# A graph network of eight layers on one core: node stages in chunks of four tiles, layer norm by the statistics instruction, batch norm in one round, counts a step later

## The reference

```python
# block 0: one layer, mean of the neighbours
agg = segment_sum(h[src], dst) / maximum(count(dst), 1)
x = x + relu(h @ W_self.T + agg @ W_neigh.T + bias)
# block 1: an edge filter, and the product of the messages at each node
bf = exp(coeff * (dist[:, None] - centers) ** 2)
bf = ssp(ssp(bf @ W1 + b1) @ W2 + b2)              # ssp(z) = softplus(z) - ln 2
msg = h[src] * edge_feat * bf * cut[:, None]
x = x + ssp(segment_prod(msg, dst) @ W3 + b3)
# block 2: three layers of  mean(h[src]) @ Wl + h @ Wr + b, relu between them
x = x + third_layer
# block 3: three attention layers, each followed by leaky relu and batch norm
out = segment_sum((h @ W)[s] * coef[:, None], d) + bias     # coef: softmax over each node's edges
h = batch_norm(leaky_relu(out, 0.01))              # mean and variance over the 6250 nodes
x = x + h
```

## Time and profile before

| | us |
|---|---|
| median of three runs | 9773.72 (9766.58 to 9774.74) |
| the profiled execution, its own time | 9773.36 |
| its span, first to last instruction | 9771.3 |
| TensorE matmuls busy | 4612.8 (47%) |
| VectorE busy | 5238.5 (54%) |
| ScalarE busy | 1189.0 (12%) |
| GpSimd busy | 6513.7 (67%) |
| mean granted TensorE clock | 0.632 of full speed |

### The profile page before, as it was taken

One profiled execution on the slowest core, in us unless ns is written; L12 is line 12 of the kernel. 1 busy time (PEld: TensorE's weight loads), 2 busy tenths in 40 slices (PEclk: granted clock), 3 DMA queues, 4 the chain that ended last, 5 costly groups with the idle time before them and its releaser, 6 DMA issues.

```text
span 9771.3 us, 95144 instructions
## 1 busy us (share of the span) xinstructions
PE 4612.8 (47%) x25947; PEld 3624.8 (37%) x25947; DVE 5238.5 (54%) x15043; ACT 1189.0 (12%) x1461; POOL 6513.7 (67%) x6626
## 2 busy tenths in 40 slices
PE   0433447777733334433443336635267353572543
PEld 0433333333333334433343335335254253442533
DVE  3455457777753333333343336957359583395844
ACT  0000017777720000000000001000010000100001
POOL 0666747777757776777677773777737777377774
PEclk9655567777765656655565555566565675655756
DMA  1211224444421122121221121233112331123321
GB/s 57 61 45 45 64 55 123 125 124 124 119 68 52 52 52 56 52 52 52 52 56 52 52 53 58 90 112 97 39 55 89 103 110 47 40 76 114 116 55 30
DMA packets 525925, 702.75 MB, mean 72 GB/s; under 512 B 121707, under 2 KB 392050, under 8 KB 524444
## 3 DMA queue, kind: packets, MB, share of 16 engines
q0 software_dynamic: 211680, 414.97, 16.3%
q1 hardware_dynamic: 299224, 230.52, 7.8%
q10 hardware_dynamic: 14688, 53.48, 1.4%
HBM read 552.58 MB, written 145.94 MB: 71 GB/s over the span
## 4 chain that ended last, share of the span: by engine, by line
POOL 52%; issue 21%; PE 13%; DVE 11%; SPq 1%; DMA 1%; ACT 0%; DVEq 0%; POOLq 0%; ACTq 0%
POOL rows L651 26%; POOL rows L681 22%; PE PS L1018 5%; DVE T L1457 2%; PE PS L1050 2%; PE PS L980 2%; POOL nd L664 1%; POOL at_first L657 1%; SPq L459 1%; DVE acc L1334 1%; PE PS L1043 1%; DVE H L1362 1%; PE PS L906 1%; DVE onehot L1316 1%; DVE H L1364 1%
## 5 line engine op out<-in xcount | busy, mean ns | idle before, releaser
L651 POOL DMA_INDIRECT rows<-table,src_t x3920 | 3899.9, 995 | 1874.7 <-issue 1216.6
L1334 DVE TENSOR_TENSOR acc<-acc,PS 128x128 f32 x5488 | 1559.6, 284 | 3383.5 <-PE PS L980 2141.2
L681 POOL DMA_INDIRECT rows<-table,src_t x2352 | 2268.5, 964 | 1137.5 <-issue 753.7
L980 PE MATMUL PS<-onehot,rows 128*128 128x128 f32 x6272 | 1451.5, 425 | 2119.2 <-DMA rows<-table,src_t 2119.2
L980 PEld LDWEIGHTS PS<-onehot,rows 128*128 128x128 f32 x6272 | 1350.3, 327 | 2208.6 <-DMA rows<-table,src_t 2208.6
L1009 PE MATMUL PS<-onehot,rows 128*128 128x128 f32 x3072 | 688.5, 415 | 1197.5 <-DMA rows<-table,src_t 1142.8
L1009 PEld LDWEIGHTS PS<-onehot,rows 128*128 128x128 f32 x3072 | 637.0, 316 | 1242.2 <-DMA rows<-table,src_t 1192.2
L1403 DVE TENSOR_SCALAR onehot<-PS,loc_t,ex_t 128x128 f32<-128x128 f32 x2352 | 943.8, 403 | 0.5
L1018 PE MATMUL PS<-H,mats 128*128 128x512 f32 x784 | 514.8, 794 | 8.9 <-DVE H L1436 6.6
L1316 DVE TENSOR_TENSOR onehot<-PS,loc_t 128x1024 f32<-128x1024 f32 x392 | 477.0, 1218 | 6.4 <-DMA table<-H 5.8
L1092 PEld LDWEIGHTS PS<-als_bf,onehot 128*128 128x128 bf16 x7056 | 308.3, 119 | 426.0 <-DVE onehot L1569 269.6
(11 more groups left out here) (308 smaller groups left out, 5372.8 us busy)
## 6 DMA issues: line engine op xcount, KB each, us to landing
rows<-table,src_t POOLq DMA_INDIRECT x6272
staged<-rows ACTq DMA_DIRECT2D x102, 512.0 KB
H<-staged SPq DMA_DIRECT2D x102, 512.0 KB
prod_rows<-onehot SPq DMA_DIRECT2D x98, 512.0 KB, 3.3
G<-in_edge_attr SPq DMA_DIRECT2D x97, 512.0 KB, 4.2
table<-H SPq DMA_DIRECT2D x49, 448.0 KB
G<-perm_rows SPq DMA_DIRECT2D x4, 3136.0 KB, 12.1
cut_row<-flat_bf SPq DMA_DIRECT2D x294, 2.0 KB
```

What stands on the lines that cost most here:

```text
L651: pool.indirect_dma_start(rows[:, j, :], None, table[k % 2], at(src_t[:, t:t + 1]))\
L681: pool.indirect_dma_start(rows[:, g % 2 * HT + j, :], None, table[k % 2], at(src_t[:, t:t + 1]))\
L980: last = mm(PS[:, o:o + D], rows[:, r, :], onehot[:, r, :], start=True, stop=True)
L1334: tt(at, at, PS[:, h * 1024 + j * D:h * 1024 + (j + 1) * D], ALU.add).then_inc(added[h], 1)
```

## The change

Four things are changed together.

1. **Chunks.** CH goes from 7 to 4, so that a chunk is 512 elements, one PSUM bank. There are 13 chunks, the last of one tile, everywhere: node stages, table stores, output stores, the node products of every layer. In the attention layers the turned rows, the products and `mid` get two buffers each, and `turn_rows(c + 1)` is issued ahead of `multiply_rows(c)`. Each layer has a semaphore of its own for its table chunks.
2. **Layer norm.** `layer_input` and the old `normalize` go. `row_moments` takes mean and variance of a tile with `bn_stats` and `bn_aggr`, one of each for every tile, on VectorE. ScalarE takes the square root of the chunk's variances, or, behind layer 1, exp(-0.5 ln v), which VectorE refines by one Newton step. VectorE makes scale and shift for each node (`shift_rows`), and ScalarE writes relu(scale * x + shift) tile by tile (`normalized_rows`). The norm of chunk c - 1 is finished behind the moments of chunk c. The input of layer 0 goes through the same chunks.
3. **Attention outputs and batch norm.** The bias is added to all of T in `self_weights`, by a second operation over it, and the self weight is divided by the softmax sum there. The output of a chunk is then a product, a sum and the leaky relu. Batch norm subtracts the mean of the first chunk in place of the mean of all nodes, sums and squares are summed on TensorE in the same round as the outputs (`first_sum`, `statistics` inside `to_nodes`), and the closing arithmetic makes scale and shift from them. A last round applies them.
4. **Counts a step later.** VectorE's digits start at step 16 instead of 15, and TensorE multiplies the digits of step c in step c + 1. Likewise the facts and the permutations move by a step.

The core of the diff:

```diff
-CH = 7
-NCH = NT // CH
+CH = 4
+NCH = -(-NT // CH)
...
-COUNT_FROM = 15
+COUNT_FROM = 16
...
+            def normalized_rows(k, c):
+                nonlocal n_norm
+                n_norm += 1
+                s.wait_ge(norm_ready, n_norm)
+                for t in tiles_of(c):
+                    last = nc.scalar.activation(H3[:, t, :], X3[:, t, :], ACT.Relu, bias=shift_n[:, t:t + 1],
+                                                scale=rstd_n[:, t:t + 1])
+                last.then_inc(h_chunks[k], 1)
...
+                    after_ranks(k, c - 1)
+                after_ranks(k, NCH - 1)
+                after_ranks(k, NCH)
+                if k in GAT:
+                    deviation(bn[:, 3 * D:4 * D], bn[:, 3 * D:4 * D])
+
+            def after_ranks(k, c):
+                if k in (0, 4):
+                    normalize(k + 1, c)
+                if k in GAT and 0 <= c < NCH:
+                    s.wait_ge(sum_in, (k - 5) * (NCH + 1) + c + 2)
+                    nc.scalar.activation(flat(G, c), flat(H, c), ACT.Square).then_inc(squares, 1)
+
+            def normalize(k, c):
+                if 0 <= c < NCH:
+                    inverse_deviation(k, c)
+                if 1 <= c <= NCH:
+                    normalized_rows(k, c - 1)
...
             def rows_product(k):
                 turn_rows(k, 0)
                 for c in range(NCH):
-                    multiply_rows(k, c)
                     if c + 1 < NCH:
                         turn_rows(k, c + 1)
+                    multiply_rows(k, c)
...
                     move_ranks(c)
+                    if k in GAT:
+                        if c == 0:
+                            first_sum(k - 5)
+                        if c > 1:
+                            statistics(k - 5, c - 2)
+                if k in GAT:
+                    statistics(k - 5, NCH - 2)
+                    statistics(k - 5, NCH - 1)
...
                     if k == 0:
-                        if COUNT_FROM <= c < FACTS_AT:
+                        if COUNT_FROM < c <= FACTS_AT:
                             for q in range(2):
-                                count_nodes(2 * (c - COUNT_FROM) + q)
-                        if c == FACTS_AT:
+                                count_nodes(2 * (c - 1 - COUNT_FROM) + q)
+                        if c == FACTS_AT + 2:
                             sum_facts()
-                        if PERM_FROM <= c < PERM_FROM + PERMS:
-                            turn_perms(c - PERM_FROM)
+                        if PERM_FROM < c <= PERM_FROM + PERMS:
+                            turn_perms(c - 1 - PERM_FROM)
...
+            def row_moments(c):
+
+                six = moments[:].rearrange("p (t q) -> p t q", q=6)
+                for j, t in enumerate(tiles_of(c)):
+                    last = nc.vector.bn_stats(six[:, j, :], X3[:, t, :])
+                step(last)
+                for j, t in enumerate(tiles_of(c)):
+                    last = nc.vector.bn_aggr(mean_var[:, t, :], six[:, j, :])
+                step(last, var_ready)
...
+            def shift_rows(c, by_log):
+                w = slice(c * CH, c * CH + len(tiles_of(c)))
+                inverse_taken()
+                if by_log:
+                    r, x, two = rstd_n[:, w], shift_n[:, w], mean_var[:, w, 1]
+                    step(stt(x, two, EPS, r, ALU.add, ALU.mult))
+                    step(stt(x, x, -0.5, r, ALU.mult, ALU.mult))
+                    step(stt(r, x, 1.5, r, ALU.add, ALU.mult))
+                else:
+                    step(recip(rstd_n[:, w], rstd_n[:, w]))
+                step(stt(shift_n[:, w], mean_var[:, w, 0], -1.0, rstd_n[:, w], ALU.mult, ALU.mult), norm_ready)
+
+            def normalize(c, by_log=False):
+                if c < NCH:
+                    row_moments(c)
+                if c > 0:
+                    shift_rows(c - 1, by_log)
...
+                step(tt(exs_n, exs_n, rden_n, ALU.mult))
                 step(tt(T3, T3, exs_n.unsqueeze(2).broadcast_to([P, NT, D]), ALU.mult))
+                step(tt(T3, T3, vec_nodes(bias_vec[k]), ALU.add))
...
+                outputs(0)
+                outputs(1)
                 v.wait_ge(sum_out, 2 * l + 1)
-                step(ts(nm, PS[:, 0:D], -1.0 / N, None, ALU.mult))
...
+                step(ts(minus_first, sums_ps, -1.0 / (CH * P), None, ALU.mult))
+                centred(0)
+                centred(1)
+                for c in range(2, NCH):
+                    outputs(c)
+                    centred(c)
                 v.wait_ge(sum_out, 2 * l + 2)
```

345 lines of the change are left out of this document (169 added, 176 removed).

## The result

The changed kernel takes 9634.7 us (median of 4 runs, 9633.54 to 9637.26) where the kernel before, run again with it, takes 9772.1: a ratio of 0.986 (95% interval 0.9843 to 0.9878). That is 137.4 us less. Predicted were 9617 (9578 to 9668) and 156.5 us less.

A forecast was written before the change was run, and what follows sets the result against it. GpSimd's gathers were taken to set the pace in the edge walks, with its idle time the rest. -90 - 17.5 - 29 - 35 + 1.5 + 13.5 = -156.5 gave 9617 us, range 9578 to 9668 (8 in 10).

The forecast's parts named there:

- Counts a step later: Layer 0's counting stretch: digits finished before TensorE's count, so GpSimd is the bound again at 10.05 us a group; -90 us.
- Statistics: Layer norm moments by bn_stats and bn_aggr on VectorE: 0.41 us for a tile, bounds 0.25 and 0.80.
- rival A: Layer 0 counts: they move and nothing is won, as VectorE's step holds the group; 9707 us, 5%.
- rival B: Layer norm statistics are dear: at 0.8 us a tile, three layers and the start grow by 76, 9693 us; 8%.
- part 2: The forecast's part on layer norm by statistics: start -17.5, layers 0 and 4 -14.5 each, layer 1 -35, layers 2 and 3 +1.5 together.
- Layers 0 and 4: Their node stages: chunks of 4.6 us, entrance 6.7, exit 6.3, 68.2 against 82.4; -14.5 us for each.
- Layer 1: Its node products: chunks of 5.2 us at the gathers' pace, no table changes, exit 6.5, 81 instead of 116.0; -35 us.
- Second pass over T: End of each attention layer: the bias pass stops GpSimd after one gather slips between the passes; +5.7 each, +17 us.
- Outputs and batch norm: Attention node stage: one round over the nodes, TensorE bound at 3.65 us a chunk, opening with first sum 10.5; -1 us (-4 to +5).
- rival D: Attention node stage: TensorE's clock falls, a chunk takes 7.2 instead of 3.65, about +40 in each of three; 9737 us, 4%.
- Row products: Attention layers: double buffers remove hand-over, granted clock stays 0.50; layer 5 -1.5 us, layers 6 and 7 -0.7 each.
- rival C: Attention row products: TensorE's clock rises from 1.2 to 2.4 GHz; -59 us, 9558 us, 12%.

The follow-up runs named there:

- run 7: Changed kernel with each tile's bn_stats taken twice: 11554.6 us against the changed kernel's 11520.8, ratio 0.9967 to the kernel before.
- run 6: Changed kernel with the old layer norm arithmetic in 13 chunks, all but the root on VectorE: ratio 1.0015 to the kernel before, 88 us over the changed kernel.
- Run 3: Changed kernel with the bias pass over T moved behind the last accumulator adds: ratio 0.9928 to the kernel before, 13 us under the changed kernel.
- run 4: Changed kernel without the first sum and the centring, sums and squares of outputs as they are: ratio 0.9912 to the kernel before, 31 us under the changed kernel.

## Why the prediction was right, point by point

The steps of it, against the profiled execution (136 us less, 156.5 forecast):

| step | forecast | measured |
|---|---|---|
| start | -17.5 | -20.7 |
| layer 0, first to last gather | -90 | -83.2 |
| gap behind layer 0 / layer 4 | -14.5 / -14.5 | -12.5 / -14.5 |
| layer 1 | -35 | -28.0, and +0.6 in its edge pass |
| gaps behind layers 2 and 3 | +0.7 / +0.7 | -1.6 / -2.4 |
| attention: second pass over T | +17 | +13.9 |
| attention: all else | -3.5 | +12.8 |

The terms that came out worse than forecast miss by 33 us together, those that came out better by 12. So the 20 us of the sum are in part misses that cancel, and that the total lies well inside the range is in part luck. One sum of the forecast is also off by a little: 82.4 less 68.2 is 14.2 for layers 0 and 4, not 14.5.

*Counts a step later.* The mechanism held: groups of 9.99 us but for the pauses, and the 90 less 5 for a cost that I did not see: a step later the store of the permutations met a pause of GpSimd's gathers. The run with the permutations moved shows that (6.6 to 7.7 us with the store beside it, 2.08 without). That the size of the gain depends on what limit comes next was in rival A only as "nothing is won"; on the slower chips this was nearly so, though not with the groups of 11.9 that A would have.

*Statistics.* 0.33 for a tile and not 0.41; rival B (0.8 and more) is out, and the doubled instruction shows how far: 0.22 us more a tile cost 34 us in all, 0.17 for each of 196 tiles. The old arithmetic in the same chunks costs 88 us, so the statistics instruction, with ScalarE's part, is what carries part 2. The start gained 3 more than forecast through this size.

*Layers 0 and 4.* 4.69 and 4.52 a chunk where 4.6 was forecast, entrance 7.2 and 6.1 (6.7), exit 6.4 (6.3). My reason for 4.6 and not VectorE's 4.3 was a loop through ScalarE. Its Relu is the smaller part: without the Relu's wait a chunk is 0.1 to 0.4 us shorter. VectorE's own work is 3.9 and not 4.3, and run 7 shows that most of what is added to it comes through. What is left, some 0.7 us a chunk, is VectorE's wait for TensorE's move. In the traces the move waits through the product for ScalarE's windows, and these stand behind a root that waits for VectorE; the product also takes 1.9 to 2.1 us in some chunks and 1.06 in others. No run parts the root's wait from the low clock. The Trainium skill (ScalarE: Activation LUTs, "Rules for kernel authors") would leave a relu on VectorE; no run tried that alone, and run 6, which moves all of the normalisation back and not only the relu, is slower.

*Layer 1.* The chunks keep the pace of the gathers, 5.3, and the table loads are gone, as forecast. The step that failed is the exit of 6.5 us. Behind the last product gather come 22.3 us, where the forecast's terms leave 15.3. When that gather ends (2661.8), the Relus of six chunks are still to come: they start at 2664.4, 2669.0, 2673.7, 2677.7 and 2679.7 (the last two in a row), and VectorE is busy for 17.4 of the 19.2 us from there to 2681. The forecast's 15.3 hold less than two chunks of 5.2 and the exit. That is the 7 us.

*Layers 2 and 3.* 1.91 a chunk, VectorE's own 1.9, where I took 2.15 by ScalarE: 12 x 0.24 = 2.9, and they came out 2.3 and 3.1 us under the forecast.

*Second pass over T.* That a gather stands until the end of the second pass was right. No gather slipped between the passes, though: the one under the first pass ended 0.8 us into the second, and the next began there. The second long gather adds 6.42 - 0.94, and the first is shorter by 7.31 - 6.42: 4.6 us in layer 5 (4.9 and 4.4 in the others), where I had 5.7. Run 3 gets 13 us back by moving the pass into a wait of VectorE.

*Outputs and batch norm.* This is the step that was mis-sized most. The chunks are right (3.57 forecast as 3.65, TensorE bound and busy throughout), the opening is not: "VectorE waits for that move once, 3 us" and 10.5 us to the first chunk behind it, where 15.5 were measured. The forecast has TensorE's wait for the first output, and with it one wait of VectorE. It misses a second one, in ScalarE's order:

```profile
7019.47 0.63 ACT L801 ACTIVATE G<-H 128x512 f32<-128x512 f32 x1 [10.53 <-DVE H L1712]
...
7020.99 2.08 PE L977 MATMUL PS<-gat_w,rows 128*128 128x128 f32 x8 [4.85 <-ACT rows L774]
```

ScalarE's square of the first chunk waits 10.5 us for the centring. The windows of a later chunk (L774) stand behind it, TensorE waits 4.9 us for them, and VectorE's third output comes 8.6 us behind the second. Meanwhile TensorE's granted clock goes down: 0.98 from 7009 to 7012, 0.50 from 7012 to 7015 and from 7021 to 7025, 0.70 over the 16 us, and its products took 1.91 and 2.08 us. That is rival D's mechanism, in the opening alone and not in the chunks behind it. The finishing round of scale and shift, 12 x 1.45 + 0.65 = 18.1 in place of 7 x 2.25 = 15.8 before the first gather of the next layer, was left out of the sum altogether: the gather waits for all chunks of the table (18.7 us from the first finished chunk, 16.7 before). Against this the idle time behind the first two groups gives back 0.9, 4.7 and 4.6 (27.27 against 31.95 in layer 6), where 1.5, 0.7 and 0.7 were forecast. In layer 6, 2.0 of the 4.7 are the gather that comes later behind the first finished chunk; the rest is the third group, released 2.7 us sooner behind it. The idle times behind the three layers grew by 6.1, 3.2 and 6.0 in all. Inside the three passes the pauses of the gathers took another 8 us; they fell at other moments than before, which the sum cannot know.

*Row products.* The clock stayed at 0.50 with TensorE busy 28.6 of 32 us, the first 28 of them without a gap, so rival C is out. The Trainium skill (TensorE: Matmul & The Clock Gate, "Part 1: The HAM clock gate") says that sustained work lifts the clock; in this stretch of these small products it did not.

## What to carry to other kernels

When work is moved a step later, list what follows it down to its last transfer, and look what that will now run beside: the cost of the counts' move was a store that met a pause. A pass that stops GpSimd belongs where VectorE waits anyway, not where it has room: at the last gathers of a layer 6.7 us of VectorE cost 4.6 of the kernel; some 20 us later, by the trace, next to nothing. And a chunked stage is priced at its ends as much as in its middle: every middle here came out within 0.25 us a chunk, and the misses were one opening, one exit and a last round that the sum left out.

## What was not expected of the hardware

GpSimd's gathers pause for 2.1 us once in 112 of them, and for 6.6 to 7.7 us at a gather of layer 0 beside which the store of 3.2 MB runs. The kernel before has it too, in its attention layers: it loads the same 3.2 MB there at 6590.0, 7847.8 and 9109.7, and pauses of 4.7, 6.7 and 7.5 us end at 6596.4, 7857.0 and 9120.2; the changed kernel has 6.5, 6.5 and 6.8 there.

On the chips of the experiments the same kernel took 11523 to 11598 us instead of 9772. Each single instruction that I compared took the same time, and the node stages too (92.1 idle before layer 1, 92.4 on the first chip); what grew were waits that no instruction on the core explains, in the edge passes (groups of 11.3 to 11.4 us and not 10.05) and for 340 us in each attention layer (6 on the first chip), in which GpSimd waited for the weighted pass to begin. So the same edit can be worth far less on another chip: some 83 us on the first chip, 15 to 18 on these.

The opening of the attention node stage had the granted clock 0.70 in the changed kernel, where TensorE waits twice, and 1.00 in run 4, without the second wait; the row products had 0.50 throughout, though TensorE worked for 28 us there without a gap.
